# First layer norm in slots 4 to 6, epsilon added on GpSimd, key minima turned by a full-width matmul, V evicted by ScalarE in two passes

## The chip, the cores and the metric

One core of a Trainium2 chip runs the whole program. Time is device microseconds (us) of one execution. Engines are named as the profile names them: PE (matmuls; PEld its weight loads), DVE (VectorE), ACT (ScalarE), POOL (GpSimd) and SP (SyncE, which issues all DMAs here).

## The reference

Two transformer layers over 16 sequences of 256 tokens, width 256, 16 heads of 16. Cut to what matters:

```python
# layer 0
t = layer_norm(x, g1, be1)                      # eps 1e-5
x = x + attention(t, t, t, key mask) @ Wo.T + bo + (ctx @ Wg.T + bg)
x = x + relu(layer_norm(x, g2, be2) @ W1.T + b1) @ W2.T + b2
# layer 1, eps 1e-6
y = causal_attention(layer_norm(x)) @ wo + x
z = attention(q from layer_norm(y), k and v from ctx) @ wo + y
out = z + relu(layer_norm(z) @ w1 + b1) @ w2 + b2
```

## The kernel before, in words

The three attentions are three **passes** (0, 1 and 2); a pass handles 16 sequences, so there are 48 tasks. The program walks through **steps**, one task each, and a step has 16 **slots**, one for each head. In a slot every engine does its piece for the head of the current task (`st.cur`) and pieces of its neighbours: the norm of the task two ahead (`st.nxt2`), the q, k and v products of the next (`st.nxt`), the output projection of the previous (`st.prev`), the MLP of the one before that (`st.old`, only passes 0 and 2). Each engine has an instruction stream of its own, in slot order and inside a slot in the order of its `slot` function; semaphores tie the streams together. So the order on every engine is written out by hand, and a wait holds up all that stands behind it in its stream.

A step goes as follows. PE makes the scores of head h into `s_ps` at the start of slot h, and for that it needs DVE's `score_guard` of head h - 2 (line 858: add the mask, take the row minimum; in pass 2 the minimum alone, line 843). Pass 0 turns the probabilities on PE (line 508). Passes 1 and 2 ("keyed") fold the minimum over each row into the product instead: POOL splits four heads' minima in three bf16 parts (`top_split`), PE turns them (`top_rows`, line 521, in slots 2, 6, 10 and 14), ACT copies them below the queries (line 729), and `keyed_scores` makes transposed scores.

The projections q and k are made by PE in slots 2 and 3, copied out by ACT, split in three bf16 parts by POOL and DVE in slots 4 to 6 (`q_f`, `k_f` are remainders, `q_part`, `k_part` the parts), written to HBM by SP (lines 381 and 390) and read back into `q_stack` and `k_stack` (lines 399 and 404). The scores of the next step cannot start before both have landed. V is made by PE in slot 10 (`V_AT`) and copied out of PSUM by DVE in slot 11 (lines 947 and 949). The MLP's first half fills slots 5 to 8 on PE; ACT evicts `h_f` (slots 6 to 9), DVE rounds `h_hi` and POOL subtracts `h_lo` (slots 7 to 10). ACT's third and fourth `h_f` wait for POOL's first and second `h_lo`, and V on PE waits for the fourth `h_f`, as they share a PSUM bank. The second half of the MLP is in slots 11, 12 and 14.

The first norm of `nxt2`: DVE takes statistics in slot 9 (line 864), aggregates and adds epsilon in slot 10 (lines 871 and 874), POOL raises to the power -0.5 (line 1095, `rstd`), and DVE normalises `x_in` in slot 12 (line 878). PE turns the result in slot 13. The second norm (of `prev`, slots 14 and 15) is built alike, with line 1098. Guards in slot h are the last thing that DVE does in it but for the copies of turned probabilities (line 994, pass 0).

## Time and profile before

| | before |
|---|---|
| median of 3 runs | 1709.86 us (1702.79 to 1710.65) |
| the profiled execution: time, span | 1704.09 us, 1702.3 us |
| busy: PE, PEld, DVE, ACT, POOL | 86%, 69%, 71%, 62%, 49% of the span |
| granted TensorE clock, mean | 0.956 |
| instructions | 42833 |

Busy shares are means over three passes whose limits differ; they say which engine is used much, not which one is waited for. A busy PE can still be a PE that pauses between slots, as the ends of its matmuls are modelled.

### The profile page before, as it was taken

The numbers are of one execution on the slowest core, as the hardware profiler recorded it, in microseconds if no ns is written. First come the engines' busy times: TensorE is split into PE (matmuls) and PEld (weight loads), VectorE is DVE, ScalarE is ACT, GpSimd is POOL, SyncE is SP. The second block draws the span as 40 slices with busy tenths as digits, with TensorE's granted clock in tenths as the row PEclk, the third lists the DMA queues.
The fourth block names the chain that finished last, engine by engine and source line by source line (L and its number), as shares of the span: only waits on it lengthen the run. The fifth ranks groups of instructions, "written<-read, shape, count | busy, mean of one in ns | idle before, by whom it ended". The sixth has DMA issues, their size and how long they took to land.

```text
span 1702.3 us, 42833 instructions
## 1 busy us (share of the span) xinstructions
PE 1459.5 (86%) x13376; PEld 1175.9 (69%) x13376; DVE 1212.1 (71%) x3855; ACT 1061.9 (62%) x2153; POOL 834.7 (49%) x1125
## 2 busy tenths in 40 slices
PE   2789999999998998878787777778999999999986
PEld 1567788877777887765566555555777777777756
DVE  2688887888878887656666766666776777677742
ACT  3677676777777775445565555556656665666552
POOL 3345454444444566544344443444555655565533
PEclk8799999999999999989899999998999999999989
DMA  5645555444544455444655646574644364546300
GB/s 145 139 113 119 108 109 118 99 99 105 117 100 99 105 125 130 119 107 107 124 121 111 129 101 140 115 153 93 119 112 105 99 128 99 105 101 129 79 26 13
DMA packets 163511, 185.75 MB, mean 109 GB/s; under 512 B 15952, under 2 KB 140240, under 8 KB 163408
## 3 DMA queue, kind: packets, MB, share of 16 engines
q1 hardware_dynamic: 163408, 184.57, 49.8%
q8 instruction: 41, 0.67, 0.2%
q14 instruction: 62, 0.51, 0.1%
HBM read 125.78 MB, written 58.72 MB: 108 GB/s over the span
## 4 chain that ended last, share of the span: by engine, by line
PE 42%; issue 13%; ACT 12%; DVE 12%; DMA 9%; POOL 6%; SPq 5%; ACTq 1%; DVEq 0%; POOLq 0%
PE d_ps L437 16%; PE d_ps L673 8%; DMA k_stack<-parts 7%; PE o_ps L572 5%; PE s_ps L494 5%; PE t_ps L542 3%; DVE prob L858 3%; PE t_ps L508 3%; SPq L399 2%; DMA parts<-q_part 2%; ACT prob_t L721 2%; SPq L404 2%; DVE o_n L890 2%; POOL h_lo L1031 2%; PE m_ps L444 1%
## 5 line engine op out<-in xcount | busy, mean ns | idle before, releaser
L721 ACT ACTIVATE prob_t<-t_ps 128x384 f32<-128x384 f32 (+1 forms) x512 | 275.4, 551 | 393.0 <-PE t_ps L542 197.7
L494 PE MATMUL s_ps<-k_stack,q_stack 96*128 96x256 bf16 (+1 forms) x1536 | 294.6, 275 | 124.5 <-DMA k_stack<-parts 47.5
L712 ACT ACTIVATE prob<-prob,neg_max 128x256 f32<-128x256 f32 x512 | 233.8, 514 | 121.0 <-DVE neg_max L858 118.8
L494 PEld LDWEIGHTS s_ps<-k_stack,q_stack 96*128 96x128 bf16 x1536 | 115.1, 100 | 227.8 <-issue 65.7
L542 PE MATMUL t_ps<-q_stack,k_stack 108*128 108x256 bf16 (+1 forms) x1024 | 207.3, 269 | 23.0 <-ACT prob_t L721 14.3
L858 DVE CUSTOM_DVE_ANT_0 prob<-s_ps,bias_sb 128x256 f32<-128x256 f32 x512 | 192.4, 416 | 48.5 <-PE s_ps L494 36.7
L858 DVE CUSTOM_DVE_ANT_0 prob<-s_ps,causal 128x128 f32<-128x128 f32 (+1 forms) x512 | 158.5, 352 | 90.2 <-PE s_ps L494 88.0
L843 DVE TENSOR_REDUCE top<-s_ps 128x2 f32<-128x512 f32 x256 | 172.9, 682 | 54.8 <-PE s_ps L494 51.3
L1031 POOL TENSOR_TENSOR h_lo<-h_f,h_hi 128x512 fp32r<-128x512 f32 x128 | 165.9, 1296 | 86.6 <-DVE h_hi L921 86.6
L572 PE MATMUL o_ps<-prob_t,v_sb 128*17 128x256 f32 (+1 forms) x3072 | 200.7, 381 | 0.0
L437 PE MATMUL d_ps<-x2t_hi,w_hi 128*128 128x256 f32 x512 | 157.0, 307 | 38.2 <-ACT k_f L780 21.8
L901 DVE STREAM_TRANSPOSE o_q<-o_ps 128x256 f32<-128x256 f32 x192 | 86.1, 449 | 133.0 <-PE o_ps L572 131.4
L508 PE MATMUL t_ps<-ident_sb,prob 128*128 128x128 f32 x1024 | 160.3, 280 | 2.5 <-DVE prob_t L994 2.0
L673 PE MATMUL d_ps<-w_hi,h_hi 128*128 128x256 f32 x512 | 148.0, 289 | 4.4 <-POOL h_lo L1031 4.4
L673 PE MATMUL d_ps<-w_hi,h_lo 128*128 128x256 f32 x512 | 147.5, 288 | 0.0
L673 PE MATMUL d_ps<-w_lo,h_hi 128*128 128x256 f32 x512 | 146.4, 286 | 0.1
L437 PE MATMUL d_ps<-x2t_lo,w_hi 128*128 128x256 f32 x512 | 145.7, 285 | 0.0
L437 PE MATMUL d_ps<-x2t_hi,w_lo 128*128 128x256 f32 x512 | 145.4, 284 | 0.0
L729 ACT ACTIVATE q_stack<-o_ps 12x1024 bf16<-12x1024 f32 x128 | 130.1, 1016 | 11.5 <-PE o_ps L521 6.7
L437 PEld LDWEIGHTS d_ps<-x2t_hi,w_hi 128*128 128x128 f32 x512 | 98.8, 193 | 52.4 <-issue 44.1
L508 PEld LDWEIGHTS t_ps<-ident_sb,prob 128*128 128x128 f32 x1024 | 121.8, 144 | 14.0 <-issue 6.6
L1031 POOL TENSOR_TENSOR x2t_lo<-tf_b,x2t_hi 128x512 fp32r<-128x512 f32 x32 | 40.9, 1277 | 181.8 <-ACT tf_b L736 181.8
(115 smaller groups left out, 4063.5 us busy)
## 6 DMA issues: line engine op xcount, KB each, us to landing
q_stack<-parts SPq DMA_DIRECT2D x288, 128.0 KB, 4.0
k_stack<-parts SPq DMA_DIRECT2D x288, 128.0 KB, 6.4
parts<-q_part SPq DMA_DIRECT2D x96, 192.0 KB, 2.3
parts<-k_part SPq DMA_DIRECT2D x96, 192.0 KB, 2.3
ct_kept<-ct_hl SPq DMA_DIRECT2D x16, 512.0 KB, 8.0
x_in<-x_mid SPq DMA_DIRECT2D x32, 256.0 KB, 2.9
x_res<-x_mid SPq DMA_DIRECT2D x32, 256.0 KB, 3.0
ct_hl<-ct_kept SPq DMA_DIRECT2D x16, 512.0 KB, 8.2
```

Source lines behind the costliest of these rows:

```text
L437: last = mm(dst, lhs, rhs, start=(opens and n == 0), stop=(closes and n == len(terms) - 1))
L494: last = mm(s_ps[:, h % 2, q * S:q * S + n], q_stack[0:ROWS, t.par, HEAD[h], q * P:(q + 1) * P], k_stack[0:ROWS, t.par, HEAD[h], 0:n], sta ...
L508: last = nc.tensor.transpose(t_ps[:, h % 2, c:c + P], prob[:, h % 4, q, k * P:(k + 1) * P], ident_sb[:, :])
L542: last = mm(t_ps[:, h % 2, k * S:k * S + S - lo], k_stack[:, t.par, HEAD[h], k * P:(k + 1) * P], q_stack[:, t.par, HEAD[h], lo:S], start=T ...
L572: last = mm(o_ps[32 * j:32 * j + VW, lo:S], v_sb[:, t.par, k, HEAD[h], :], prob_t[:, h % 8, k * S:k * S + S - lo], start=(k == 0), stop=(k ...
L673: last = mm(d_ps[:, 0, t * D:(t + 1) * D], lhs, rhs, start=(f == 0 and n == 0), stop=(f == FT - 1 and n == 2))
L712: last = nc.scalar.activation(prob[:, h % 4, q, :], prob[:, h % 4, q, :], ACT.Exp, bias=neg_max[:, h % 4, q:q + 1], scale=-1.0)
L721: nc.scalar.activation(prob_t[:, h % 8, 0:n], t_ps[:, h % 2, 0:n], ACT.Exp, scale=-1.0)\
L729: nc.scalar.activation(rows, o_ps[ROWS:ROWS + TOP, S:2 * S].unsqueeze(1).to_broadcast([TOP, CH, S]), ACT.Copy).then_inc(top_row.sem, 1)
L843: v.tensor_reduce(top[:, h // CH % 2, :, h % CH], s_ps[:, h % 2, :].rearrange("p (q k) -> p q k", q=TT), AX_X, ALU.min).then_inc(u_done.se ...
L858: last = v.tensor_tensor_reduce(prob[:, h % 4, q, 0:n], s_ps[:, h % 2, q * S:q * S + n], bias, 1.0, HUGE, ALU.add, ALU.min, least)
L1031: g.tensor_tensor(dst, a, b, ALU.subtract).then_inc(done, 1)
```

## The change

Six edits. The first norm's three pieces on DVE move from slots 9, 10 and 12 to slots 4, 5 and 6, and POOL's `rstd` from slot 10 to slot 5. Epsilon is added by POOL from a small table, in both norms, not by DVE. In pass 0 the output's norm moves from slots 6 and 7 to 7 and 8. The minima are turned by a matmul of 108 weight columns (96 of zeros, then the 12 wanted) without a tile position, not by one of 12 columns at column 96. V is evicted in passes 1 and 2 by one ACT instruction in place of two of DVE. The causal mask is one 128x256 tile, read at an offset.

```diff
-NORM_AT = (6, 10, 10)
+NORM_AT = (7, 10, 10)
+STATS_AT, MEAN_AT, HAT_AT = 4, 5, 6
...
+        eps_sb = sb("eps_sb", [P, NPASS, TT])
-        top_part = sb("top_part", [P, 2, TT, CH, NSPLIT], BF16)
+        top_wide = sb("top_wide", [P, 2, TT, ROWS + TOP], BF16)
...
-                    last = mm(o_ps[ROWS:ROWS + TOP, S + q * P:S + (q + 1) * P],
-                              top_part[:, c % 2, q].rearrange("p j n -> p (j n)"), ident_bf[:, :],
-                              start=True, stop=True, tile_position=(0, ROWS))
+                    last = mm(o_ps[0:ROWS + TOP, S + q * P:S + (q + 1) * P], top_wide[:, c % 2, q, :], ident_bf[:, :],
+                              start=True, stop=True)
...
+                if h == V_AT + 1 and has(st.nxt, KEYED):
+                    act.wait_ge(v_mm.sem, v_mm.after(st.nxt))
+                    if st.prev:
+                        act.wait_ge(pv_mm.sem, pv_mm.after(st.prev))
+                    act.sem_inc(passed, 1)
+                    nc.scalar.activation(v_sb[:, st.nxt.par, :, :, 0:HD],
+                                         d_ps[:, 1, :].rearrange("p (k h d) -> p k h d", k=TT, d=HD), ACT.Copy)\
+                        .then_inc(v_done.sem, 1)
...
-                dve.wait_ge(mv_done.sem, mv_done.after(task))
-                v.tensor_scalar(ve_t[:, :], mv_t[:, :, 1], eps, None, ALU.add).then_inc(ve_done.sem, 1)
...
-                if h == 9 and has(st.nxt2):
+                if h == STATS_AT and has(st.nxt2):
...
-                if h == 10 and has(st.nxt2):
+                if h == MEAN_AT and has(st.nxt2):
...
-                if h == V_AT + 1 and has(st.nxt):
+                if h == V_AT + 1 and has(st.nxt, (0,)):
...
-                if h == 12 and has(st.nxt2):
+                if h == HAT_AT and has(st.nxt2):
...
-                if h == 10 and has(st.nxt2):
+                if h == MEAN_AT and has(st.nxt2):
+                    pool.wait_ge(ln_mv.sem, ln_mv.after(st.nxt2))
+                    pool.sem_inc(passed, 1)
+                    g.tensor_tensor(ve[:, :], mv[:, :, 1], eps_sb[:, st.nxt2.p], ALU.add).then_inc(ln_ve.sem, 1)
                     pool.wait_ge(ln_ve.sem, ln_ve.after(st.nxt2))
                     if st.nxt:
                         pool.wait_ge(x_hat.sem, x_hat.after(st.nxt))
                     g.tensor_tensor(rstd[:, :], ve[:, :], minus_half[:, :], ALU.pow).then_inc(ln_rstd.sem, 1)
```

POOL's stream in the loop over pass 0, slots 4 to 7, before (line 1031 is the helper `sub`; `ct_hl` belongs to the gate's context, `h_lo` to the MLP):

```order
L1031 TENSOR_TENSOR q_f<-q_f,q_part 128x512
L1031 TENSOR_TENSOR k_f<-k_f,k_part 128x512
L1031 TENSOR_TENSOR q_part<-q_f,q_part 128x512
L1031 TENSOR_TENSOR k_part<-k_f,k_part 128x512
L1074 REGISTER_ALU
L1031 TENSOR_TENSOR ct_hl<-tf_b,ct_hl 128x512
```

The same stretch of POOL's stream in the changed kernel, where `sub` is line 1038:

```order
L1038 TENSOR_TENSOR q_f<-q_f,q_part 128x512
L1038 TENSOR_TENSOR k_f<-k_f,k_part 128x512
L1038 TENSOR_TENSOR q_part<-q_f,q_part 128x512
L1100 REGISTER_ALU
L1102 TENSOR_TENSOR ve<-mv,eps_sb 128x2
L1106 TENSOR_TENSOR rstd<-ve,minus_half 128x2
L1038 TENSOR_TENSOR k_part<-k_f,k_part 128x512
```

Two small operations now stand between the third and the fourth of the splits. They stood behind the MLP's subtractions before.

DVE's stream in the same loop, slots 5 and 6, before (the `ISA` rows are the guard, two of a kind for each half of the head; the second halves are left out):

```order
L914 CAST q_part<-q_f 128x512
L841 REGISTER_ALU
L858 ISA prob,neg_max<-s_ps,bias_sb 128x256
...
L885 RECIPROCAL rden<-o_q 128x32
L886 REGISTER_ALU
L888 REGISTER_ALU
L890 TENSOR_TENSOR o_n<-o_q,rden 128x2x8x16 x2
L917 CAST k_part<-k_f 128x512
L841 REGISTER_ALU
L858 ISA prob,neg_max<-s_ps,bias_sb 128x256
```

The same slots of DVE's stream in the changed kernel:

```order
L921 CAST q_part<-q_f 128x512
L877 REGISTER_ALU
L880 BN_AGGR mv<-stats 128x2 x2
L850 REGISTER_ALU
L867 ISA prob,neg_max<-s_ps,bias_sb 128x256
...
L924 CAST k_part<-k_f 128x512
L885 TENSOR_SCALAR x_in<-x_in,mv,rstd 128x256 x2
L850 REGISTER_ALU
L867 ISA prob,neg_max<-s_ps,bias_sb 128x256
```

The output's norm (reciprocal and `o_n`) has left the place ahead of the cast of `k_part`; the normalisation of `x_in` has come in between that cast and the guard of head 6.

## Rows read from the trace of the kernel before

**Rows 1.** Windows, three passes: busy us (instructions) by engine, PEclk, DMA share, GB/s

```profile
140.00:560.00 420.00, 384.52 (x3505) 333.40 (x3496) 347.96 (x1131) 306.28 (x710) 202.27 (x170) 1.00 0.48 107
700.00:1040.00 340.00, 271.13 (x2752) 204.46 (x2754) 224.99 (x1028) 188.97 (x348) 153.17 (x289) 0.92 0.56 119
1120.00:1600.00 480.00, 443.35 (x3970) 344.59 (x3959) 343.22 (x683) 305.87 (x557) 267.16 (x419) 0.99 0.51 109
```

**Rows 2.** Timeline of the DMA queue in the second pass: start, us, what

```profile
740.91 0.40 SPq L370 DMA_DIRECT2D x_res<-x_mid  x1
...
818.78 0.40 SPq L414 DMA_DIRECT2D x_mid<-x  x1
...
1033.95 0.38 SPq L370 DMA_DIRECT2D x_res<-x_mid  x1
```

**Rows 3.** Chain that ended last, second pass: start, us, what

```profile
813.42 8.86 DMA k_stack<-parts
...
843.14 5.78 DMA k_stack<-parts
```

**Rows 4.** Timeline of PE, second pass; in brackets idle before and releaser

```profile
795.05 0.34 PE L494 MATMUL s_ps<-k_stack,q_stack 96*128 96x128 bf16 x2 [2.08 <-DMA k_stack<-parts]
...
802.86 0.33 PE L494 MATMUL s_ps<-k_stack,q_stack 96*128 96x128 bf16 x2
...
803.12 0.28 PE L521 MATMUL o_ps<-ident_bf,top_part 128*12 128x128 bf16 x2
...
803.33 0.28 PE L542 MATMUL t_ps<-q_stack,k_stack 108*128 108x256 bf16 x1
...
806.31 0.34 PE L494 MATMUL s_ps<-k_stack,q_stack 96*128 96x128 bf16 x2 [1.10 <-DVE top L858]
...
806.49 0.27 PE L542 MATMUL t_ps<-q_stack,k_stack 108*128 108x256 bf16 x1
...
822.40 0.50 PE L494 MATMUL s_ps<-k_stack,q_stack 96*128 96x128 bf16 x2 [3.98 <-DMA k_stack<-parts]
```

**Rows 5.** Timeline of POOL, the same step

```profile
804.27 1.15 POOL L1031 TENSOR_TENSOR q_part<-q_f,q_part 128x512 bf16<-128x512 f32 x1
...
805.78 1.16 POOL L1031 TENSOR_TENSOR k_part<-k_f,k_part 128x512 bf16<-128x512 f32 x1 [0.36 <-DVE k_part L917]
...
806.90 0.21 POOL L1043 TENSOR_TENSOR top_part<-top,zeros 128x8 bf16<-128x8 f32 x1
...
811.07 0.69 POOL L1095 TENSOR_TENSOR rstd<-ve,minus_half 128x2 f32<-128x2 f32 x1 [3.11 <-DVE ve L874]
```

**Rows 6.** Timeline of DVE, the same step

```profile
804.34 1.36 DVE L917 CAST k_part<-k_f 128x512 bf16<-128x512 f32 x1 [0.49 <-POOL k_f L1031]
```

**Rows 7.** Timeline of DVE, one step of the first pass

```profile
391.50 0.42 DVE L858 CUSTOM_DVE_ANT_0 prob<-s_ps,bias_sb 128x256 f32<-128x256 f32 x1 [1.32 <-PE s_ps L494]
...
397.11 1.39 DVE L917 CAST k_part<-k_f 128x512 bf16<-128x512 f32 x1
...
398.41 0.41 DVE L858 CUSTOM_DVE_ANT_0 prob<-s_ps,bias_sb 128x256 f32<-128x256 f32 x1
...
407.59 1.20 DVE L874 TENSOR_SCALAR ve<-mv 128x2 f32<-128x2 f32 x1
...
411.33 1.05 DVE L878 TENSOR_SCALAR x_in<-x_in,mv,rstd 128x256 f32<-128x256 f32 x2
```

**Rows 8.** Timeline of POOL, the same step of the first pass

```profile
396.86 1.34 POOL L1031 TENSOR_TENSOR q_part<-q_f,q_part 128x512 bf16<-128x512 f32 x1
```

**Rows 9.** Timeline of ACT, the same step of the first pass

```profile
405.55 0.84 ACT L805 ACTIVATE h_f<-d_ps,cols_sb 128x256 f32<-128x256 f32 x2 [0.79 <-POOL h_lo L1031]
```

**Rows 10.** Timelines of ACT and of PE, one step of the third pass

```profile
1364.49 0.84 ACT L805 ACTIVATE h_f<-d_ps,cols_sb 128x256 f32<-128x256 f32 x2
...
1370.44 0.39 PE L494 MATMUL s_ps<-k_stack,q_stack 96*128 96x256 bf16 x2 [0.31 <-DVE top L843]
```

**Rows 11.** Groups of instructions by line: count, busy us, mean ns, idle before

```profile
L874 DVE TENSOR_SCALAR ve<-mv 128x2 f32<-128x2 f32 x80 | 42.3, 529 | 2.7
```

More of the change, by code:

```diff
@@ L209, in two_layers @@
         bias_sb = sb("bias_sb", [P, 2, TT, S])
-        causal = sb("causal", [P, TT, S])
+        causal = sb("causal", [P, S])
         s_ps = es.enter_context(nc.psum_tensor("s_ps", [P, 2, 512], F32))
@@ L855, in score_guard @@
                     n = (q + 1) * P if t.p == 1 else S
-                    bias = causal[:, q, 0:n] if t.p == 1 else bias_sb[:, t.par, q, 0:n]
+                    bias = causal[:, S - n:S] if t.p == 1 else bias_sb[:, t.par, q, 0:n]
                     least = top[:, h // CH % 2, q, h % CH:h % CH + 1] if t.p == 1 else neg_max[:, h % 4, q:q + 1]
@@ L865, in statistics, with aggregate @@
                 last.then_inc(done.sem, 1)
-            def aggregate(task, st_t, mv_t, ve_t, eps, stats_done, mv_done, ve_done):
+            def aggregate(task, st_t, mv_t, stats_done, mv_done):
                 dve.wait_ge(stats_done.sem, stats_done.after(task))
@@ L936, in slot @@
                         dve.wait_ge(ln_rstd.sem, ln_rstd.after(st.nxt))
[L937 to L938 removed]
+                    aggregate(st.nxt2, stats, mv, ln_stats, ln_mv)
+                if h == V_AT + 1 and has(st.nxt, (0,)):
                     dve.wait_ge(v_mm.sem, v_mm.after(st.nxt))
@@ L944, in slot @@
                         src = d_ps[:, 1, k * D:(k + 1) * D].rearrange("p (h d) -> p h d", d=HD)
-                        if st.nxt.p == 0:
-                            bv = rows_sb[:, R_BV, :].rearrange("p (h d) -> p h d", d=HD)
-                            last = v.tensor_tensor(dst, src, bv, ALU.add)
-                        else:
-                            last = v.tensor_copy(dst, src)
+                        bv = rows_sb[:, R_BV, :].rearrange("p (h d) -> p h d", d=HD)
+                        last = v.tensor_tensor(dst, src, bv, ALU.add)
                     last.then_inc(v_done.sem, 1)
-                if h == 12 and has(st.nxt2):
+                if h == HAT_AT and has(st.nxt2):
                     dve.wait_ge(ln_rstd.sem, ln_rstd.after(st.nxt2))
@@ L974, in slot @@
                         dve.wait_ge(ln2_rstd.sem, ln2_rstd.after(st.old))
-                    aggregate(t, stats2, mv2, ve2, LN_EPS[t.p], ln2_stats, ln2_mv, ln2_ve)
+                    aggregate(t, stats2, mv2, ln2_stats, ln2_mv)
                 if h == 15 and has(st.prev, MLP):
@@ L1010, in _ @@
             g.memset(minus_half[:, :], -0.5).then_inc(causal_made, 1)
-            g.memset(causal[:, :, :], 0.0).then_inc(causal_made, 1)
+            g.memset(causal[:, :], 0.0).then_inc(causal_made, 1)
             pool.wait_ge(causal_made, 2)
-            g.affine_select(out=causal[:, :, :], in_=causal[:, :, :], compare_op=ALU.is_ge, fill=MASKED, base=0,
-                            pattern=[[P, TT], [-1, S]], channel_multiplier=1).then_inc(causal_made, 1)
+            g.affine_select(out=causal[:, :], in_=causal[:, :], compare_op=ALU.is_ge, fill=MASKED, base=P,
+                            pattern=[[-1, S]], channel_multiplier=1).then_inc(causal_made, 1)
             g.memset(later[:, :], 0.0).then_inc(causal_made, 1)
@@ L1020, in _ @@
             g.memset(zeros[:, :, :], 0.0).then_inc(zeroed, 1)
-            pool.wait_ge(zeroed, 1)
+            g.memset(top_wide[:, :, :, :], 0.0).then_inc(zeroed, 1)
+            for p in range(NPASS):
+                g.memset(eps_sb[:, p], LN_EPS[p]).then_inc(zeroed, 1)
+            pool.wait_ge(zeroed, 2 + NPASS)
             pool.wait_ge(const_landed, 48)
@@ L1041, in top_split @@
                     pool.wait_ge(top_mm.sem, top_mm.after(before, cb + 1))
-                src, part = top[:, c % 2], top_part[:, c % 2]
+                src = top[:, c % 2]
+                part = top_wide[:, c % 2, :, ROWS:].rearrange("p q (j n) -> p q j n", n=NSPLIT)
                 g.tensor_tensor(part[:, :, :, 0], src, zeros[:, :, :], ALU.add).then_inc(top_1.sem, 1)
@@ L1096, in slot @@
                 if h == 14 and has(st.prev, MLP):
+                    pool.wait_ge(ln2_mv.sem, ln2_mv.after(st.prev))
+                    pool.sem_inc(passed, 1)
+                    g.tensor_tensor(ve2[:, :], mv2[:, :, 1], eps_sb[:, st.prev.p], ALU.add).then_inc(ln2_ve.sem, 1)
                     pool.wait_ge(ln2_ve.sem, ln2_ve.after(st.prev))
```

1 line of the change is left out of this document (removed).

## The prediction

> **What bounds the kernel now.** I read the windows of the three passes first [rows 1]. In the first and third, PE is busy 384.5 of 420 us and 443.4 of 480 us at a granted clock of 1.00 and 0.99; what can be won there is a few short pauses in each step. In the second it is busy 271 of 340 us at 0.92: something else sets the pace. The chain that ended last names it: after the last read of `k_stack` is issued at 813.42, 8.86 us pass until it has landed, elsewhere 5.78 us [rows 3], and PE's scores at 822.40 come after 3.98 us of idling, released by that transfer [rows 4]. This is a loop: scores, then q and k, then their splitting on ACT, POOL and DVE, then two trips through HBM, then the scores of the next step. Eleven steps pass between the issues of `x_res` at 740.91 and 1033.95 [rows 2]: 26.6 us each.
>
> Why does the same read take 8.86 us in one step and 5.78 in another? The store of `x_mid` is issued at 818.78 [rows 2], 5.4 us into the long landing, with `x_in` and `x_res` behind it; a landing of 5.78 us would be all but over by then. A PE that runs early starts the neighbours' transfers early, on top of the one it will wait for. Being later at the end of a step can therefore be nearly free in this pass.
>
> In the first pass I read one step engine by engine. DVE is idle 1.32 us before the guard at 391.50 [rows 7], in slot 4, and then has hardly a gap until slot 12. Its guards pace PE there.
>
> **Part by part.**
>
> Epsilon. The add on DVE takes 529 ns on average over 80 [rows 11], but 1.20 us in slot 10 of pass 0 [rows 7], where it began while POOL was subtracting. On POOL it is a new instruction on 128x2; the nearest row is 0.21 us on 128x8 [rows 5], the upper bound by rows is the 0.69 us of the power next to it [rows 5]. I take 0.25 us with its wait.
>
> Statistics to slot 4. Two instructions, 0.7 us, go into the idle 1.32 us before the guard of slot 4 [rows 7]: nothing. If `x_in` landed late they would hold DVE; it is issued at the start of the step, and four slots lie between.
>
> Aggregate to slot 5: 0.3 us ahead of the guard of head 5. PE does not wait for that guard now.
>
> Normalise to slot 6. Here a new wait comes in. `rstd` is queued on POOL behind the subtractions of `k_f` and `q_part`. In pass 1 `q_part` runs from 804.27 for 1.15 us, to 805.42 [rows 5]; add 0.25 for epsilon and 0.69 for the power [rows 5], with the wait between them: 806.45. DVE has cast `k_part` by 805.70 (804.34 + 1.36) [rows 6] and stands still for 0.75 us. When `rstd` is there, POOL goes straight on to subtract `k_part` (1.16 us [rows 5]), a moment before DVE can start. Two normalising instructions that overlap a POOL subtraction took 1.05 us together in pass 0 [rows 7]; the epsilon add took 1.20 us where its mean is 529 ns [rows 11], and it too began beside one. Ending 0.45 us after POOL (806.5 + 1.15 + 0.45), DVE is free at 808.0 and the guard of head 6 starts 2.4 us later than now. Without the overlap it would be 1.6 us.
>
> The Trainium skill (SBUF — State Buffer, "Who interferes with whom") says of this that VectorE's copies, casts and tensor_scalars in a two-port mode and GpSimd exclude each other for a whole instruction, and that whoever issues first wins. By that rule the normalisation loses to `k_part`, and the later of my two numbers holds; the cast that took 1.36 us beside `q_part` [rows 6] agrees with it.
>
> The same in pass 0: `q_part` ends at 396.86 + 1.34 [rows 8], a little sooner when DVE no longer disturbs it, say 398.0; `rstd` at 399.0; DVE free at 400.65 where the guard of head 6 began at 398.41 [rows 7], 2.2 us later. The output's norm, which filled the wait for `k_f` before the cast at 397.11 [rows 7], now comes behind this guard and holds up the next two. Who waits? ACT's exponentials stand in its stream ahead of the MLP's evictions, POOL's first two `h_lo` come after DVE's casts, and ACT's fourth `h_f`, which POOL's `h_lo` releases at 405.55 [rows 9], moves to about 407.0. V on PE needs it. I estimate 1.2 us of delay of PE in slot 11 (1.45 less what V had in hand), and from there to the step's end PE is dense. DVE gets back 0.7 + 0.3 + 1.2 + 1.05 us in slots 9, 10 and 12, but by slot 12 it only comes out even. So +1.2 us for each of 14 steps and the two that follow with an MLP of pass 0: 16 x 1.2 = +19.2 us. Bounds: +0.2 if the normalisation wins its port, +1.7 if nothing is regained behind V.
>
> Pass 2: the same wait makes the guard 2.4 us late; the fourth `h_f` (1364.49 now [rows 10]) waits for the second `h_lo`, to about 1366.2, and V starts 1.3 us late. PE's idle 0.31 us before the scores at 1370.44 [rows 10] and about 0.2 near it go away, since statistics and epsilon have left slots 9 and 10: +0.8. Bounds -0.3 to +1.
>
> The turned minima. Without a turn between them, the scores at 806.31 are followed by keyed scores at 806.49, 0.18 us later; with one, 802.86 to 803.12 is 0.26 us, and the two small matmuls hold PE until 803.33, 0.21 us for 256 columns, where the 384 columns of the scores before 806.49 passed in 0.18, or 0.12 for 256 [rows 4]. That is 0.08 to 0.1 us on either side of each turn, 0.2 us x 4 in a step. In slots 2, 6 and 10 PE waits soon afterwards for ACT or DVE, so in pass 2 I count slot 14 alone: -0.2. Pass 2 then gives 14 x 0.6 = +8.4 us. Bounds for this edit: 0 and 128 x 0.2 = 25.6 us.
>
> The Trainium skill (TensorEngine Tiling (Array Packing), "Key Properties") says that changing the tiling mode drains TensorE. By that rule each turn stops costing two drains and all 25.6 us could come; the pauses in [rows 4] agree in kind.
>
> V on ACT: DVE's two copies go from slot 11, where in pass 2 nothing waits for DVE; ACT has idle time before PE asks for V's bank in slot 14. Nothing. The mask and the second norm's epsilon: nothing.
>
> Pass 1. The guard of head 6 is 2.4 us late, and PE's 1.10 us wait for it at 806.31 [rows 4] becomes about 3.4. Later pauses for DVE in slots 11 to 13 disappear. The DMA loop gains 0.2 by the turn in slot 2 and loses 0.25, as `k_part` ends 0.75 us later and SP issues its write before the reads of `q_stack`. What remains is when the landing ends. If PE comes to the end of its step a little later, the store at 818.78 moves behind it, and a landing of 5.78 us gives a step of 813.4 + 5.8 - 795.05 [rows 4] = 24.2 us; with collisions it stays at 26.6. I take 25.2, as the long pause will also bring stretches at the lower clock: 14 x -1.4 = -19.6 us.
>
> **Sum.** 1704.1 (the profiled execution; the median of the three runs is 5.8 above) + 19.2 + 8.4 - 19.6 = 1712 us. About 0.5%, 8.5 us, is what a measurement of this kernel can tell from no change.
>
> **Rivals.**
>
> Faster: the wait for `rstd` is absorbed. For it speaks that DVE has many gaps in pass 2 and that the chain there runs through the statistics and the epsilon add in slots 9 and 10; against it, how few gaps it has in pass 0. From 1.0 us of delay of the guard downwards nobody waits. Then pass 0 gives 0, pass 2 14 x -0.3 - 14 x 0.2 = -7, pass 1 -19.6: 1677 to 1685, say 1682. Chance 0.20.
>
> Faster by the turn: the pauses around the turns are on the path nearly everywhere, -25.6 with the forecast's other terms: 1712 + 2.8 - 25.6 = 1689. Chance 0.10.
>
> Slower: pass 1 does not repay. The 3.4 us pause in slots 7 and 8 drops the clock, as the half-pace stretch behind the 3.98 us at 822.40 shows (0.50 us for a pair that takes 0.34 at 806.31 [rows 4]); PE itself becomes the bound at today's 26.6 us. It decides from a loss of 1.4 us a step: 1704.1 + 27.6 = 1732. Chance 0.28.
>
> **How the numbers follow.** The forecast has the remaining 0.42, with a range of its own from 1700 to 1724: 0.27 of it within 0.5%, 0.13 above, 0.02 below. Faster: 0.20 + 0.10 + 0.02 = 0.32. Same: 0.27. Slower: 0.28 + 0.13 = 0.41. The range of 1680 to 1738 leaves out half of the first rival and the top of the third.
>
> **What would show it.** DVE idle before the normalisation in slot 6, released by POOL's `rstd`, some 0.75 us; the normalisation at over 1 us; PE's wait in slot 8 of pass 1 at about 3 us; landings of `k_stack` near 6 us and steps near 25 us there; V in pass 0 released by `h_f` later than now; no pause on either side of the turned minima. The prediction is wrong if DVE reaches the guard of head 6 at the old distance from the step's start, or if the steps of pass 1 keep their length.

## The result, and the profile after

The changed kernel takes 1755.97 us (median of 4 runs, 1755.04 to 1760.80) beside 1706.32 us for the kernel before on the same chip: a ratio of 1.030, interval 1.026 to 1.034. It is slower by 3%. The profiled execution took 1755.3 us, span 1753.5, mean clock 0.939.

The page gives first the busy time of each engine, and then the group of ACT's exponentials: instruction, count, busy us, mean ns, then idle time before them and its releaser. The last line is that group in the kernel before.

```profile
PE 1457.8 (83%) x13376; PEld 1191.2 (68%) x13376; DVE 1207.8 (69%) x3711; ACT 1074.4 (61%) x2185; POOL 850.0 (48%) x1209
...
L713 ACT ACTIVATE prob<-prob,neg_max 128x256 f32<-128x256 f32 x512 | 233.5, 514 | 153.5 <-DVE neg_max L867 151.7
```

```profile
L712 ACT ACTIVATE prob<-prob,neg_max 128x256 f32<-128x256 f32 x512 | 233.8, 514 | 121.0 <-DVE neg_max L858 118.8
```

Every engine is busy for a smaller share than before. ACT's exponentials (L713) wait 151.7 us for the minima of DVE's guards, where they waited 118.8 us; so DVE's guards come later.

Windows inside the three passes: window, length, then busy us (instructions) of PE, PEld, DVE, ACT, POOL, clock, DMA share, GB/s.

```profile
140.00:560.00 420.00, 375.18 (x3320) 320.26 (x3319) 327.67 (x1057) 288.92 (x668) 197.23 (x184) 0.98 0.46 103
737.00:1077.00 340.00, 264.14 (x2648) 208.70 (x2648) 224.45 (x971) 185.65 (x347) 151.80 (x287) 0.86 0.55 115
1170.00:1650.00 480.00, 423.89 (x3869) 339.60 (x3870) 333.11 (x616) 305.83 (x560) 268.25 (x439) 0.98 0.52 107
```

Against [rows 1] PE does less in the same time in all three, and the second pass runs at 0.86. To see where the time went I take the issues of `x_res`, one for each task, as milestones. The timeline of the changed kernel's SP has the first and the seventeenth at:

```profile
81.96 0.46 SPq L372 DMA_DIRECT2D x_res<-x  x1
...
731.08 0.40 SPq L372 DMA_DIRECT2D x_res<-x_mid  x1
```

These are 649.1 us for the sixteen steps of pass 0. The same milestones of every kernel (pass 1 from the 19th issue to the 33rd, 14 steps; pass 2 from the 35th to the 48th, 13 steps), with the measured ratio to the kernel before on the chip of that run:

| kernel | ratio (95% interval) | first issue | pass 0 | pass 1 | pass 2 |
|---|---|---|---|---|---|
| before | 1 | 76.1 | 619.7 | 378.0 | 438.4 |
| before, once more | (one run) | 79.7 | 618.5 | 377.5 | 440.0 |
| changed | 1.030 (1.026 to 1.034) | 82.0 | 649.1 | 385.2 | 446.4 |
| normalise in 12 | 1.009 (1.006 to 1.012) | 79.3 | 621.1 | 402.0 | 434.3 |
| slots 9, 10, 12 | 0.988 (0.984 to 0.992) | 78.2 | 615.4 | 387.9 | 428.9 |
| the same again | 0.990 (0.986 to 0.993) | 78.0 | 615.4 | 388.2 | 428.7 |
| norm of O in 6 | 1.028 (1.024 to 1.032) | 82.5 | 657.5 | 390.8 | 446.4 |
| slots alone | 1.028 (1.023 to 1.032) | 82.5 | 651.4 | 385.7 | 448.6 |
| turns alone | 0.998 (0.996 to 1.000) | 78.8 | 617.1 | 387.8 | 438.1 |
| V on ACT alone | 1.001 (0.999 to 1.003) | 77.7 | 618.0 | 391.2 | 439.1 |
| epsilon alone | 0.997 (0.994 to 0.999) | 78.3 | 618.2 | 392.0 | 431.6 |
| root behind k_part, norm. 12 | 0.996 (0.994 to 0.998) | 78.5 | 617.3 | 400.1 | 434.9 |
| epsilon and turns | 0.992 (0.989 to 0.995) | 77.6 | 615.3 | 376.2 | 428.0 |
| normalise in 7 | 1.027 (1.023 to 1.031) | 78.3 | 645.6 | 394.4 | 443.7 |
| k_part held | 1.031 (1.027 to 1.034) | 83.0 | 633.6 | 406.8 | 443.6 |
| root first | 1.021 (1.016 to 1.026) | 81.5 | 626.1 | 398.4 | 449.4 |
| statistics in 4 alone | 0.992 (0.987 to 0.997) | 80.6 | 611.6 | 384.8 | 427.4 |
| slots 9, 10, 12, norm of O in 6 | 0.994 (0.992 to 0.997) | 79.6 | 618.8 | 388.5 | 427.8 |

Passes 0 and 2 repeat to 2 us between executions (the first two rows, and the pair in rows five and six). The start moves by 3.6 us between two executions of one kernel. Pass 1 agrees to 0.5 us within each of these two pairs, but it must vary too: the execution profiled of "root behind k_part" took 1722 us, where the median of its twelve runs is 1707.7, and "V on ACT alone" has 391.2 in pass 1 at a ratio of 1.001. So I read passes 0 and 2 from single profiles, and for pass 1 trust ratios more.

Of the changed kernel's 51 us of span, 29.4 are in pass 0 (1.8 us a step), 7.2 in pass 1, 8.0 in pass 2, 5.9 in the start; the two passages between the passes and the end add 0.7. The 7.2 of pass 1 is not clear of variation. The start is 81.5 to 83.0 us in all five kernels that normalise in slot 6, and 76.1 to 80.6 us in the thirteen others, so part of the 5.9 seems to go with that slot; nothing here shows how.

**Pass 0.** DVE in one step of the changed kernel: guard of head 5, the cast of `k_part`, the normalisation, guard of head 6.

```profile
414.73 0.42 DVE L867 CUSTOM_DVE_ANT_0 prob<-s_ps,bias_sb 128x256 f32<-128x256 f32 x1
...
416.52 1.37 DVE L924 CAST k_part<-k_f 128x512 bf16<-128x512 f32 x1 [1.36 <-POOL k_f L1038]
...
418.75 2.54 DVE L885 TENSOR_SCALAR x_in<-x_in,mv,rstd 128x256 f32<-128x256 f32 x2 [0.86 <-POOL rstd L1106]
...
421.21 0.41 DVE L867 CUSTOM_DVE_ANT_0 prob<-s_ps,bias_sb 128x256 f32<-128x256 f32 x1
```

POOL's timeline of the same stretch:

```profile
416.44 1.16 POOL L1038 TENSOR_TENSOR q_part<-q_f,q_part 128x512 bf16<-128x512 f32 x1
...
417.56 0.38 POOL L1102 TENSOR_TENSOR ve<-mv,eps_sb 128x2 f32<-128x2 f32 x1
...
418.02 0.69 POOL L1106 TENSOR_TENSOR rstd<-ve,minus_half 128x2 f32<-128x2 f32 x1
...
418.67 1.16 POOL L1038 TENSOR_TENSOR k_part<-k_f,k_part 128x512 bf16<-128x512 f32 x1
...
419.79 1.34 POOL L1038 TENSOR_TENSOR ct_hl<-tf_b,ct_hl 128x512 fp32r<-128x512 f32 x1
```

DVE waits 0.86 us for the root, and then its two normalising instructions take 2.54 us: they overlap not one subtraction but two, `k_part` and right behind it `ct_hl`. From guard 5 to guard 6 it is 421.21 - 414.73 = 6.5 us; before it was 398.41 - 394.73 = 3.7 us (398.41 in [rows 7], 394.73 from the same timeline). PE:

```profile
415.38 0.35 PE L439 MATMUL d_ps<-x2t_hi,w_hi 128*128 128x256 f32 x1 [1.69 <-ACT k_f L781]
...
422.03 0.39 PE L496 MATMUL s_ps<-k_stack,q_stack 96*128 96x256 bf16 x2 [0.86 <-DVE neg_max L867]
...
422.72 0.63 PE L510 MATMUL t_ps<-ident_sb,prob 128*128 128x128 f32 x4 [0.30 <-DVE prob_t L998]
...
423.69 0.39 PE L439 MATMUL d_ps<-x2t_hi,w_hi 128*128 128x256 f32 x1 [0.34 <-ACT h_f L806]
...
425.26 1.06 PE L573 MATMUL o_ps<-prob_t,v_sb 128*17 128x256 f32 x16
```

The scores of slot 8 are the first to suffer (0.86 us), then the turn (0.30) and the MLP behind `h_f` (0.34). From the first product here to the `o_ps` of slot 8 it is 425.26 - 415.38 = 9.88 us.

**Pass 1.** PE around a turn, and at the scores that wait for guard 6:

```profile
921.64 0.33 PE L496 MATMUL s_ps<-k_stack,q_stack 96*128 96x128 bf16 x2
...
921.82 0.32 PE L523 MATMUL o_ps<-ident_bf,top_wide 128*108 128x128 bf16 x2
...
922.04 0.28 PE L543 MATMUL t_ps<-q_stack,k_stack 108*128 108x256 bf16 x1
...
927.50 0.50 PE L496 MATMUL s_ps<-k_stack,q_stack 96*128 96x128 bf16 x2 [3.51 <-DVE top L867]
```

The wait is 3.51 us where [rows 4] had 1.10, and the half pace (0.50 us for a pair) follows it. At this turn the pause ahead is gone (921.64 to 921.82 is 0.18 us, in [rows 4] 0.26), that behind it is not (0.22 us, then 0.21). Of the four turns in a step of pass 1 this is the only one with keyed scores behind it. In pass 2 both pauses are gone. PE around a turn there, before (slot 10), then changed (slot 6):

```profile
1297.31 0.38 PE L494 MATMUL s_ps<-k_stack,q_stack 96*128 96x256 bf16 x2
1297.62 0.28 PE L521 MATMUL o_ps<-ident_bf,top_part 128*12 128x128 bf16 x2
1297.83 0.39 PE L437 MATMUL d_ps<-w_hi,ct_hl 128*128 128x256 f32 x1
```

```profile
1298.92 0.38 PE L496 MATMUL s_ps<-k_stack,q_stack 96*128 96x256 bf16 x2
1299.14 0.28 PE L523 MATMUL o_ps<-ident_bf,top_wide 128*108 128x128 bf16 x2
1299.22 0.36 PE L439 MATMUL d_ps<-x2t_hi,w_hi 128*128 128x256 f32 x1
```

From the scores to the turn it is 0.31 us, then 0.22; from the turn to the next product 0.21, then 0.08. SP in the step of pass 1:

```profile
924.30 0.90 SPq L383 DMA_DIRECT2D parts<-q_part  x2
...
926.51 0.89 SPq L392 DMA_DIRECT2D parts<-k_part  x2
...
940.09 0.40 SPq L416 DMA_DIRECT2D x_mid<-x  x1
```

`k_part` is written 2.2 us behind `q_part`; before it was 1.5 us in the median of eleven steps. A landing of `k_stack` that stands in the chain:

```profile
932.76 8.98 DMA k_stack<-parts
```

It is as long as the long one in [rows 3], though the store of `x_mid` is issued 940.09 - 932.76 = 7.3 us into it and not 5.4. Over the sixteen steps of the second pass the median landing is 7.8 us in the changed kernel, and 7.0 and 7.4 in the two executions of the kernel before. In the execution that the prediction was read from, the store is issued 5.2 to 5.4 us into six of them, and these take 5.3, 5.3, 5.8, 6.9, 8.9 and 9.2 us: the same collision goes with short landings and long ones.

**Pass 2.** ACT's `h_f` in the window 1220 to 1600 us, before and changed, and PE's product for V in slot 10 of the changed kernel:

```profile
L805 ACT ACTIVATE h_f<-d_ps,cols_sb 128x256 f32<-128x256 f32 x92 | 38.6, 475 | 0.3
```

```profile
L806 ACT ACTIVATE h_f<-d_ps,cols_sb 128x256 f32<-128x256 f32 x88 | 37.0, 475 | 24.8 <-POOL h_lo L1038 23.3 <-PE d_ps L439 1.2
...
1308.72 0.39 PE L439 MATMUL d_ps<-w_hi,ct_hl 128*128 128x256 f32 x1 [1.17 <-ACT h_f L806]
```

ACT now waits for POOL's `h_lo`, and V on PE waits 1.17 us for ACT's fourth `h_f`; the same product at 1297.83 in the kernel before waited for nothing. So in this pass PE loses its time in slot 10, on the path that the prediction named.

The normalisation in the three passes (windows 180 to 560, 780 to 1060, 1220 to 1600 us: count, busy us, mean ns of one, idle time before and releaser):

```profile
L885 DVE TENSOR_SCALAR x_in<-x_in,mv,rstd 128x256 f32<-128x256 f32 x18 | 22.8, 1307 | 7.7 <-POOL rstd L1106 7.7
L885 DVE TENSOR_SCALAR x_in<-x_in,mv,rstd 128x256 f32<-128x256 f32 x20 | 15.5, 814 | 8.5 <-POOL rstd L1106 8.5
L885 DVE TENSOR_SCALAR x_in<-x_in,mv,rstd 128x256 f32<-128x256 f32 x22 | 17.2, 819 | 9.4 <-POOL rstd L1106 9.4
```

### The profile page after: what moved, and what is told of

Same layout as the page of the kernel before. It is cut to its first block, busy times and chain, and to the rows that moved or that the text cites. A ratio compares the mean times of both kernels' runs of the same rounds, so it can differ in the third digit from the quotient of the medians.

```text
span 1753.5 us, 42890 instructions
## 1 busy us (share of the span) xinstructions
PE 1457.8 (83%) x13376; PEld 1191.2 (68%) x13376; DVE 1207.8 (69%) x3711; ACT 1074.4 (61%) x2185; POOL 850.0 (48%) x1209
## 4 chain that ended last, share of the span: by engine, by line
PE 35%; issue 22%; POOL 14%; DVE 12%; ACT 7%; DMA 5%; SPq 3%; DVEq 1%; POOLq 0%; ACTq 0%
PE d_ps L439 13%; PE d_ps L674 7%; PE o_ps L573 5%; DMA k_stack<-parts 5%; PE s_ps L496 4%; DVE prob L867 3%; PE t_ps L543 2%; PE t_ps L510 2%; POOL q_part L1038 2%; POOL q_f L1038 2%; POOL k_part L1038 2%; POOL rstd L1106 1%; SPq L401 1%; DVE x_in L885 1%; ACT h_f L806 1%
## 5 line engine op out<-in xcount | busy, mean ns | idle before, releaser
L713 ACT ACTIVATE prob<-prob,neg_max 128x256 f32<-128x256 f32 x512 | 233.5, 514 | 153.5 <-DVE neg_max L867 151.7
L573 PE MATMUL o_ps<-prob_t,v_sb 128*17 128x256 f32 (+1 forms) x3072 | 208.0, 393 | 0.0
L439 PEld LDWEIGHTS d_ps<-x2t_hi,w_hi 128*128 128x128 f32 x512 | 102.4, 200 | 63.0 <-issue 45.1
L543 PEld LDWEIGHTS t_ps<-q_stack,k_stack 108*128 108x128 bf16 x1024 | 89.3, 102 | 65.9 <-ACT prob_t L722 38.6
```

The costliest lines, as they stand in the source:

```text
L439: last = mm(dst, lhs, rhs, start=(opens and n == 0), stop=(closes and n == len(terms) - 1))
L543: last = mm(t_ps[:, h % 2, k * S:k * S + S - lo], k_stack[:, t.par, HEAD[h], k * P:(k + 1) * P], q_stack[:, t.par, HEAD[h], lo:S], start=T ...
L573: last = mm(o_ps[32 * j:32 * j + VW, lo:S], v_sb[:, t.par, k, HEAD[h], :], prob_t[:, h % 8, k * S:k * S + S - lo], start=(k == 0), stop=(k ...
L713: last = nc.scalar.activation(prob[:, h % 4, q, :], prob[:, h % 4, q, :], ACT.Exp, bias=neg_max[:, h % 4, q:q + 1], scale=-1.0)
```

## The experiments

### The slots: all back, the normalisation back, or the slots alone

```diff
-STATS_AT, MEAN_AT, HAT_AT = 4, 5, 6
+STATS_AT, MEAN_AT, HAT_AT = 4, 5, 12
```

> The changed kernel with its normalisation put back to slot 12; statistics stay in slot 4, the aggregate, eps and reciprocal root in slot 5. First theory: the normalisation in slot 6 waits for the reciprocal root (0.85 us) and then shares the port with GpSimd's subtractions (1.55 us in place of 0.46; 2.54 in pass 0), and the guard of head 6 behind it is what delays every step. Then this run gives back about 40 of the 50 us: 1708 to 1720 us, the pass-0 step goes from 41.6 back to at most 39.8 us, the pass-1 step from 27.4 to at most 26.8. Rival: eps and the reciprocal root ahead of GpSimd's k_part subtraction in slot 5 lengthen the road to the k_part DMAs. Then the time stays at 1745 us or more and k_part is still issued 2.2 us behind q_part.

Measured: 1731.76 us, 1.009. Passes 0 and 2 are back (621.1 and 434.3), so the first theory held for these, with 2 points of the 3. The time is 12 us above its range, and most of that is the chip, on which the kernel before took 1717.57 us and not 1706.32. The rival was right about the rest: `k_part` is still written 2.2 us behind `q_part`, and pass 1 is the longest seen so far. PE in this run, pass 0, from the same product to the same `o_ps`:

```profile
400.76 0.36 PE L439 MATMUL d_ps<-x2t_hi,w_hi 128*128 128x256 f32 x1 [1.69 <-ACT k_f L781]
...
408.58 1.06 PE L573 MATMUL o_ps<-prob_t,v_sb 128*17 128x256 f32 x16
```

That is 7.82 us, 2.06 less than in the changed kernel: the loss of a step stands entirely in this stretch.

In the second pass, PE's waits from 800 to 1030 us (us in total, times, longest), the changed kernel first, this run second:

```profile
PE s_ps L496 <- DVE top L867: 30.6, 16, 3.5
PE s_ps L496 <- DMA k_stack<-parts: 9.8, 5, 2.2
```

```profile
PE s_ps L496 <- DMA k_stack<-parts: 42.2, 9, 5.8
PE s_ps L496 <- DVE top L867: 11.3, 16, 1.1
```

The waits for the guard have turned into waits for the landing: in pass 1 the two hide each other.

```diff
-STATS_AT, MEAN_AT, HAT_AT = 4, 5, 6
+STATS_AT, MEAN_AT, HAT_AT = 9, 10, 12
```

> The changed kernel with all three parts of the first norm back in slots 9, 10 and 12; eps on GpSimd, the turned minima and V on ScalarE stay. First theory: the slots carry the whole loss, so 1700 to 1712 us. Rival: one of the other three edits carries a part of it; then 1720 us or more, with the part to be looked for in runs of one edit each. Against the run with the normalisation alone put back: a difference of over 8 us says that the statistics in slot 4 or the root in slot 5 also cost.

Measured: 1698.16 us, 0.988. The slots carry the whole loss and a little more: without them the other edits gain 1.2%. Between this and the run above lie 2 points, which the statistics in slot 4 or the aggregate and the root in slot 5 must carry.

The kernel before with the slots alone (9, 10 and 12 to 4, 5 and 6 in DVE's and POOL's functions, nothing else):

> The kernel before with only the first norm moved to slots 4, 5 and 6; eps stays on VectorE, the minima keep their tile position, V stays on VectorE. First theory: this alone makes the loss, 1740 to 1765 us, with a pass-0 step of 41 us or more and the normalisation in slot 6 at 1.5 us or more. Rival: the loss needs the other edits too (eps on GpSimd puts 0.4 us more ahead of the root); then under 1725 us.

Measured: 1765.16 us, 1.028, pass 0 at 651.4, pass 2 at 448.6 us. The first theory, without help from any other edit.

```diff
-NORM_AT = (7, 10, 10)
+NORM_AT = (6, 10, 10)
```

> The changed kernel with the norm of O in pass 0 back in slot 6 in place of 7. The normalisation of x stays in slot 6 of all passes. Theory that the normalisation in slot 6 is the cause: the pass-0 step stays above 41 us, the whole within 8 us of 1756, or slower, since slot 6 then holds both norms. Rival: the norm of O a slot later delays the h_f transposes and the write of the second half; then pass 0 goes back to 39.8 us or less a step and the whole to about 1727 us.

Measured: 1768.27 us, 1.028, pass 0 at 657.5 us. The norm of O in slot 7 does not cost; with both norms in slot 6 pass 0 is 8 us longer. The rival falls.

### The small edits alone

Each is the kernel before with that hunk of the diff alone (the single causal tile goes with the turns).

> The kernel before with only the minima turned without tile position (and the one causal tile that goes with it). With the slots of the first norm put back, the changed kernel was 1.2% faster than the kernel before, so one of its three small edits earns something; its third pass took 33.08 us a step in place of 33.99. Theory A, the turns: four turns a step, 0.08 us each as the trace of the changed kernel shows, 0.3 us a step in all three passes: 10 to 15 us faster, a ratio of 0.991 to 0.994, third pass 33.6 to 33.7 us a step. Theory B, the prediction's: 0.2 us a step where PE sets the pace, the third pass alone: a ratio of 0.997 to 1.000.

Measured: 1713.36 us, 0.998 (0.996 to 1.000). Theory A falls. The ratio is B's, but not its place: pass 2 is unchanged (438.1). The pauses are gone all the same. From one head's scores to the next's on PE, averaged over twelve steps of pass 2, the slots with a turn (2, 6, 10 and 14) are 0.22 to 0.24 us shorter than before; the slots 0, 4, 7 and 11 behind them are 0.19 to 0.23 us longer. What a turn frees, PE spends waiting soon afterwards.

> The kernel before with only V evicted by ScalarE in the second and third pass. Theory A: VectorE, which the guards of the scores wait on, is freed of two copies of 0.42 us a step; 0.5 to 0.6 us a step come out in the third pass and little in the second, which waits for a landing: 8 to 15 us faster, a ratio of 0.991 to 0.995, the first pass unchanged at 39.3 to 39.4 us. Theory B, the prediction's: nothing, 0.998 to 1.002, since ScalarE takes up 0.59 us in the same slot.

Measured: 1717.62 us, 1.001. The prediction's "nothing" holds.

> The kernel before with only eps added by GpSimd, in slots 10 and 14. The prediction priced it at nothing on the path: a ratio of 0.998 to 1.002. Rival: the sum stood on VectorE right behind the aggregate and held up the guard of the next head by 0.2 to 0.5 us a step; then 0.3 us times 48, a ratio of 0.990 to 0.993, in all three passes alike.

Measured: 1710.24 us, 0.997 (0.994 to 0.999). Neither as written: nothing in pass 0, but 431.6 in place of 438.4 and 440.0 us in pass 2, 0.5 to 0.6 us a step. Before, in pass 2, DVE's add and POOL's subtraction next to it:

```profile
1232.62 1.20 DVE L874 TENSOR_SCALAR ve<-mv 128x2 f32<-128x2 f32 x1
```

```profile
1232.51 1.28 POOL L1031 TENSOR_TENSOR h_lo<-h_f,h_hi 128x512 fp32r<-128x512 f32 x1 [1.35 <-DVE h_hi L921]
```

A 128x2 addition takes 1.20 us since it begins 0.11 us after a 128x512 subtraction of POOL and ends as that ends. Over the window 1220 to 1600 us of the kernel before, then the same addition on POOL in this run (slot 10):

```profile
L874 DVE TENSOR_SCALAR ve<-mv 128x2 f32<-128x2 f32 x22 | 15.1, 685 | 0.8
```

```profile
L1095 POOL TENSOR_TENSOR ve<-mv,eps_sb 128x2 f32<-128x2 f32 x11 | 2.1, 195 | 0.0
```

DVE's stream is rid of 1.2 us there in slot 10, right ahead of a guard, and POOL takes on 0.2. PE's stretch from the scores of slot 11 to those of slot 12 falls from 2.85 to 2.34 us, and this is most of the gain.

### The small edits together

The kernel with all three and the slots at 9, 10 and 12, again:

> The changed kernel with all three parts of the first norm back in slots 9, 10 and 12, measured again with more rounds. Alone, the three small edits gave 0.9984 (turns), 1.0008 (V) and 0.9966 (eps): together 0.9958 if they add. If they do no more than add, 0.993 to 0.998 here; if they help one another, 0.986 to 0.991 again, with the third pass at 33.1 us a step.

Measured: 1699.31 us, 0.990 (0.986 to 0.993), the range of the second case. But this kernel holds a fourth small edit, the norm of O in slot 7. With that back in slot 6 the same three give 0.994 (0.992 to 0.997; the last run below), which is hardly more than their sum of 0.996, and pass 0 is 3.4 us longer. So most of what is won beyond the sum goes with the norm of O, which no run tried alone. In pass 2 the three do help one another a little: 428.7 us again, against 431.6 with epsilon alone.

The same with V back on DVE:

> The kernel before with eps on GpSimd and the turned minima, V left on VectorE, norm in slots 9, 10, 12. If V on ScalarE is worth nothing, this equals the version with all three small edits (within 0.2%, third pass 33.1 us a step). If V is what brings that version from 33.28 (eps alone) to 33.08 us, this stays at 33.2 to 33.3 us and a ratio 0.2 to 0.5% above it.

Measured: 1699.67 us, 0.992 (0.989 to 0.995), pass 2 at 428.0. V on ACT is worth nothing here either. Beside epsilon on POOL the turns bring pass 2 from 431.6 to 428.0, 0.3 us a step; alone they gave 0. The place shows why: the stretch from slot 11 to slot 12, which gave back the turn of slot 10 when they stood alone (3.04 us), is 2.28 us here, since the addition no longer stands ahead of the guard.

> The kernel before, unedited, once more: how far its passes vary from one execution to another. If the variation lies in the landings of the second pass, the first and third pass repeat to 0.1 us a step (39.4 and 34.0) and the second comes out at 26.8 to 28 us a step; a start of 76 to 79 us would say that part of the changed kernel's 5.9 us at the start is variation too.

Measured: 1708.15 us, with start, pass 0, 1 and 2 at 79.7, 618.5, 377.5 and 440.0. The start moved by 3.6 us, to just above the expected range. Pass 1 is 27.0 us a step both times, so this pair shows no variation in it.

### What it is in slot 6: the wait, the shared port, or the place

One slot later (`HAT_AT` 7):

> The changed kernel with the normalisation one slot later, 7 in place of 6; statistics and root stay in slots 4 and 5. The root has then long been there, and in the second and third pass GpSimd's k_part subtraction is about over, while in the first pass the ct_lo subtraction and the norm of O still stand in the same place. If the wait and the shared port in slot 6 make the loss: third pass back to 33.7 us a step, first pass 39.5 to 40.5 us, a ratio of 1.005 to 1.015, near that of slot 12 (1.009). If the loss comes from having the normalisation anywhere in the front half, in which the k_part road runs: still over 1.02.

Measured: 1756.13 us, 1.027. The first expectation was wrong and the second held: no wait for the root is left in passes 0 and 2, and the time is hardly better. The rows of the normalisation there (the window of pass 1 left out):

```profile
L885 DVE TENSOR_SCALAR x_in<-x_in,mv,rstd 128x256 f32<-128x256 f32 x18 | 15.3, 888 | 0.0
...
L885 DVE TENSOR_SCALAR x_in<-x_in,mv,rstd 128x256 f32<-128x256 f32 x22 | 18.6, 884 | 0.0
```

In slot 7 it meets POOL's `h_lo` (884 to 888 ns where 410 is the undisturbed time), so it is slower than in slot 6 in pass 2 and faster in pass 0, and the guard behind it is late all the same. In pass 0 slot 7 also holds the norm of O. In pass 2 the normalisation now stands ahead of DVE's second rounding `h_hi`, and ACT's fourth `h_f` waits 1.5 us a step for the `h_lo` behind it, where it waited 1.0 us in the changed kernel: V is as late as before.

GpSimd's subtraction held until the normalisation is through:

```diff
                 if h == 6 and has(st.nxt):
+                    if has(st.nxt2):
+                        pool.wait_ge(x_hat.sem, x_hat.after(st.nxt2))
                     pool.wait_ge(k_p2.sem, k_p2.after(st.nxt))
                     sub(k_part[:, 2], k_f[:, :, :], k_part[:, 1], k_p3.sem)
```

> The changed kernel, with GpSimd's k_part subtraction held until the normalisation in slot 6 is through. Port theory: the two instructions then take about 0.8 us in place of 1.55 (2.54 in the first pass), and the guard of head 6 comes 0.7 to 1.7 us sooner; the first pass falls from 41.5 to 40 to 40.8 us a step, the third from 34.7 to 34.2 or less, while the second may lose, as k_part is 1.6 us later: 1735 to 1750 us in all, a ratio of 1.015 to 1.025. Wait theory: it is the wait for the root and the place that count, and the ratio stays at 1.027 or more.

Measured: 1771.01 us, 1.031. In the whole the wait theory's figure, but in passes 0 and 2 the port theory's:

```profile
L885 DVE TENSOR_SCALAR x_in<-x_in,mv,rstd 128x256 f32<-128x256 f32 x18 | 6.6, 411 | 7.7 <-POOL rstd L1108 7.7
L885 DVE TENSOR_SCALAR x_in<-x_in,mv,rstd 128x256 f32<-128x256 f32 x20 | 7.4, 410 | 8.5 <-POOL rstd L1108 8.5
L885 DVE TENSOR_SCALAR x_in<-x_in,mv,rstd 128x256 f32<-128x256 f32 x22 | 8.1, 410 | 9.4 <-POOL rstd L1108 9.4
```

410 ns in all three passes, from 1307, 814 and 819, with the wait of 0.85 us unchanged. Pass 0 gets 15.5 us back, pass 2 2.8 us. Pass 1 pays 21.6 us: `k_part` is now written 3.1 us behind `q_part`, 0.9 us later, and a step is 1.5 us longer.

POOL's epsilon and root moved up in its stream, ahead of the `k_f` subtraction of slot 5:

> The changed kernel with eps and the root on GpSimd put ahead of the k_f subtraction in slot 5. The wait of 0.85 us before the normalisation goes, but k_f and the cast of k_part behind it come about 1.1 us later and the sharing with the k_part subtraction stays. Wait theory: the loss falls by a third or more, a ratio of 1.020 or less. Road theory: GpSimd carries the same work in the same stretch in either order, and the guard of head 6 is as late as before: 1.025 to 1.035.

Measured: 1750.77 us, 1.021 (1.016 to 1.026), between the two theories and nearer the first: the loss falls by 0.9 of its 3.0 points. The wait is gone, and in pass 0 the normalisation is faster:

```profile
L885 DVE TENSOR_SCALAR x_in<-x_in,mv,rstd 128x256 f32<-128x256 f32 x18 | 14.2, 826 | 0.0
```

Pass 0 gets 23 us back. Pass 2 pays 3.0: DVE's cast waits for the late `k_f`, where it waited 0.0 us in the changed kernel:

```profile
L924 DVE CAST k_part<-k_f 128x512 bf16<-128x512 f32 x11 | 15.0, 1367 | 19.0 <-POOL k_f L1038 19.0
```

Pass 1 pays 13 us. So the wait and the sharing each make a part of the loss of pass 0, and neither can be removed on POOL without paying on the road of q and k.

### What the root in slot 5 costs by itself

Normalisation in slot 12, statistics in 4, aggregate in 5; POOL's epsilon and root moved behind the `k_part` subtraction of slot 6:

> The changed kernel with the normalisation in slot 12, statistics in 4 and the aggregate in 5, but eps and the root on GpSimd put behind the k_part subtraction of slot 6. With the root ahead of that subtraction the second pass took 28.5 us a step, against 27.7 with all three parts in slots 9, 10 and 12. Theory: the root ahead of the subtraction holds k_part, the reads of q_stack and k_stack and the scores back (the k_part store is issued 2.2 us behind that of q_part, not 1.5). Then this run has k_part 1.5 us behind q_part again, 27.7 us or less in the second pass, and a ratio of 0.986 to 0.992. Rival: the statistics in slot 4 or the aggregate in slot 5 cost it on VectorE; then the second pass stays at 28.3 us or more and the ratio at 1.005 or more.

Measured: 1707.70 us (twelve runs), 0.996, where the order ahead of the subtraction gave 1.009. `k_part` is 1.5 us behind `q_part` again. The rival falls; the expectation held in kind, with a ratio a little above its range. The profiled execution is the slowest of the twelve, so its pass 1 (400 us) doesn't count as evidence. That the gain stands in pass 1 is therefore only inferred: pass 0 gives 3.8 us of it and pass 2 nothing.

Statistics in slot 4, aggregate, epsilon and root in 10, normalisation in 12:

> The changed kernel with statistics in slot 4, aggregate, eps and root in 10, normalisation in 12. If the root ahead of the k_part subtraction made the 2% between the version with the normalisation in slot 12 (1.0089) and that with all parts put back (0.988 to 0.990), this run is at 0.986 to 0.993. If the statistics in slot 4 made it, 1.003 or more.

Measured: 1703.01 us, 0.992 (0.987 to 0.997). The statistics in slot 4 cost nothing; the aggregate, epsilon and root in slot 5 make the difference to 1.009, and 1.3 points of it are the place of epsilon and root ahead of the `k_part` subtraction. The rest is seen in pass 2, 427.4 us here against 434.3 and 434.9 in the two runs with the root early: in the window 1220 to 1600 us ACT's `h_f` waits 0.9 us in all here and 9.9 and 12.4 us there, nearly all for POOL's `h_lo`. Early, the root stands ahead of the MLP's subtractions too.

### A better version

Slots 9, 10 and 12 and the norm of O in slot 6:

> The changed kernel with the first norm in slots 9, 10 and 12 and, new, the norm of O of the first pass back in slot 6, where it fills VectorE's wait of 1.36 us for k_f. If VectorE's guards of heads 6 to 8 pace PE in the first pass, 0.3 to 0.8 us a step come out: first pass 38.5 to 38.9 us in place of 39.2, a ratio of 0.980 to 0.987. If PE is dense behind them anyway, the same as with the norm of O in slot 7: 0.987 to 0.991.

Measured: 1707.72 us, 0.994 (0.992 to 0.997). Neither as written: pass 0 is not shorter but 3.4 us longer (618.8 against 615.4), and there PE waits 3.1 us for ACT's `h_f` in the window 180 to 560 us, a wait that the version with the norm of O in slot 7 does not have. The best version is the one measured twice, all small edits, the norm of O in slot 7 among them, with the slots left at 9, 10 and 12: 0.988 and 0.990. It beats both kernels, and differs from the changed one in one line.

## Why the prediction was wrong

The forecast was 1712 us, 43 us below the profiled execution. Term by term, forecast and measured: pass 0 +19.2 and +29.4, pass 1 -19.6 and +7.2, pass 2 +8.4 and +8.0, start 0 and +5.9, the rest 0 and +0.7.

**Pass 1 (the step that failed).** "If PE comes to the end of its step a little later, the store at 818.78 moves behind it", and the landing was to be 5.78 us; that gave the term of -1.4 us a step. The store did move, to 7.3 us into the landing, and the landing stayed at 8.98 us; a step took 27.5 us and not 25.2. The collision of the store with the landing was read out of two landings, and the other landings of the same trace speak against it (5.3 to 9.2 us at one and the same distance of the store). What makes them long is open. Where landings ended PE's waits for less time (9.8 us in the window 800 to 1030 us, 14.7 before), its waits for the guards grew (30.6 us, 21.5 before). The price put on `k_part` ("gains 0.2 by the turn in slot 2 and loses 0.25") was too small as well: 0.9 us more on that road came with 1.5 us a step where it was tried, in one profiled execution, and epsilon and root ahead of the `k_part` subtraction, with the normalisation out of the way, made 1.3% (1.009 against 0.996). Why the run with the normalisation in 12 has a longer pass 1 than the changed kernel, with the same road, is open too. The third rival (1732 us, "pass 1 does not repay") named what is seen, the half pace behind a pause of 3.4 us included; measured 3.51, with a granted clock of 0.86 in the pass for 0.92. That PE itself is the bound there is not shown, since it still waits for landings and guards. The rival was too low, as it kept the forecast's pass 0 and start.

**Normalise in slot 6, pass 0.** The delay of DVE came as forecast: wait 0.86 us (forecast 0.75), port lost to POOL. The path from there to PE did not, and the term was mis-sized at 1.2 us a step, measured 1.8. Only `k_part` was counted, where the `ct_hl` subtraction stands right behind it in POOL's stream, shown among the rows on the change; the pair took 2.54 us and guard 6 came 2.8 us later than before, not 2.2. And the delay was looked for behind ACT's fourth `h_f` in slot 11; PE lost it in slot 8 already, at its own scores, which stand two slots behind the guard. The upper bound of 1.7 fell short as well. That the MLP's stretch from slot 11 is dense and gives nothing back was right.

**Pass 2.** Forecast +0.8 for the slots, measured in the run of the slots alone 448.6 - 438.4 = 10.2 us in 13 steps, +0.8. The path was right too: `h_lo`, the fourth `h_f`, then V on PE, which waits 1.17 us (1.3 was forecast). The turns were counted at -0.2, for slot 14 alone; beside slots at 9, 10 and 12 and epsilon on POOL they give 0.3, and all small edits beside the slots of the change give 0.2 at most (446.4 us against 448.6 with the slots alone).

**Epsilon.** The cost on POOL was put at 0.25 us, measured 0.20 (slots 10 and 14) to 0.38 (slot 5). The gain was missed: [rows 7] showed 1.20 us for the addition, and it was counted among what DVE gets back, not as time ahead of a guard. In the kernel before it is worth 0.5 us a step of pass 2. Beside the slots of the change no gain shows (1.030 with it, 1.028 without). The addition has then left slot 10 in any case: in the run of the slots alone it took 1.07 us in slot 5 of pass 2, beside POOL's `q_part` subtraction, and PE's stretch from slot 11 to slot 12 was already down at 2.38 us.

**The turned minima.** The pauses went, and were sized rightly: in pass 2 the stretch from the second matmul of the scores to the second of the next product falls from 0.63 to 0.39 us in the median, where 0.2 was forecast for a turn. What failed is the rival's condition that they are on the path: 0.998 alone, far from 25.6 us. That PE waits soon afterwards was forecast for slots 2, 6 and 10; it holds for slot 14 as well. By the Trainium skill (TensorEngine Tiling (Array Packing), "Key Properties") each change of tiling mode drains TensorE, and both pauses would go; the trace agrees for both, but for the turn with keyed scores behind it (0.22 us, 0.21 before).

**Statistics, V, mask.** Nothing each, as forecast: 0.992 with the statistics in slot 4 beside 0.988 and 0.990 without, intervals overlapping, and 1.001 for V. The aggregate was priced at nothing, and the root's place ahead of `k_part` at 0.25 us; the root's place cost more.

**The shared port.** The Trainium skill (SBUF — State Buffer, "Who interferes with whom") says that two-port VectorE operations and GpSimd exclude each other for a whole instruction. This case agrees, with 410 ns held apart and 814 to 1307 ns together, and also for an operation of two elements a partition (1.20 us). The prediction's 1.05 us for two normalisations [rows 7] was read as beside a subtraction; POOL's instruction there, at 410.63 for 1.27 us, adds the bias to `x` (L1089).
